# The delta rule's output projection in three fp32r products of split weights and split rows

## The reference, cut to what matters

```python
g = (hs @ Wg + bg).reshape(Bn, Ln, H, DV)
o = o * jax.lax.rsqrt(jnp.mean(o * o, axis=-1, keepdims=True) + EPS)
o = o * onorm_w * _silu(g)
o = o.reshape(Bn, Ln, H * DV) @ Wo + bo
...
x = x + _L0_attn_ref(_layernorm(x, axis=-1), ...)
```

## Time and profile before

| | us |
|---|---|
| median of 3 runs | 2178.61 |
| lowest and highest of them | 2173.72, 2178.92 |
| time of the profiled execution | 2174.62 |
| its span, from first to last instruction | 2172.6 |

### The profile page before, as it was taken

The page is one execution under the profiler, slowest core; times in us unless marked ns, Lnnn a source line. Parts: engine busy times, 40 slices in busy tenths (PEclk is TensorE's granted clock), DMA queues, the critical chain, the costliest instruction groups (busy, mean ns, idle before and its releaser), DMA issues. The chain is left out here.

```text
span 2172.6 us, 22255 instructions
## 1 busy us (share of the span) xinstructions
PE 1700.4 (78%) x7383; PEld 1173.6 (54%) x7383; DVE 1178.3 (54%) x2499; ACT 689.4 (32%) x1388; POOL 90.6 (4%) x262
## 2 busy tenths in 40 slices
PE   5999999999987999930940005971999999999993
PEld 2577777777765777720310004551666666666662
DVE  2233344333432258899999993332655555555553
ACT  1222222222212454430000003111555555555551
POOL 0000000000000000000211110002000000000003
PEclk9999999999987999975975556985999999999997
DMA  2100000000003234552200005205551554054104
GB/s 89 30 23 22 22 26 25 22 22 22 22 0 120 65 51 49 82 81 53 97 0 0 0 0 147 53 1 202 204 179 35 179 179 165 35 179 165 35 15 126
DMA packets 116295, 153.30 MB, mean 71 GB/s; under 512 B 47025, under 2 KB 67889, under 8 KB 116209
## 3 DMA queue, kind: packets, MB, share of 16 engines
q1 hardware_dynamic: 110336, 137.81, 21.9%
q0 software_dynamic: 2560, 8.39, 1.2%
q10 hardware_dynamic: 3312, 6.03, 0.7%
HBM read 250.58 MB, written 31.39 MB: 130 GB/s over the span
## 5 line engine op out<-in xcount | busy, mean ns | idle before, releaser
L1399 DVE TENSOR_TENSOR gl<-w_gu,gh 128x2048 fp32r<-128x2048 f32 x138 | 290.7, 2107 | 34.5 <-ACT gh L1346 34.5
L1346 ACT CAST gh<-w_gu 128x2048 fp32r<-128x2048 f32 x138 | 242.2, 1755 | 64.6 <-DMA w_gu<-in_up_proj 54.6
L1311 PE MATMUL bank<-w_d,hT 128*128 128x512 f32 x506 | 242.1, 597 | 9.3 <-ACT hT L1370 9.3
L1288 PE MATMUL bank<-gh,xh 128*128 128x512 f32 (+1 forms) x552 | 219.5, 398 | 12.1 <-DVE xl L1390 11.9
L1290 PE MATMUL bank<-gh,xl 128*128 128x512 f32 (+1 forms) x552 | 207.3, 376 | 0.0
L1289 PE MATMUL bank<-gl,xh 128*128 128x512 f32 (+1 forms) x552 | 206.3, 374 | 0.0
L964 PE MATMUL bank<-o_v,o_outw 128*128 128x64 f32 x256 | 36.3, 311 | 215.4 <-DMA o_v<-scratch_v_rows 215.4
L1413 DVE TENSOR_TENSOR hid<-silu,bank 128x256 f32<-128x256 f32 x138 | 55.1, 399 | 263.0 <-ACT silu L1359 262.8
L309 PE MATMUL bank<-ctxT,xa_wkv 128*128 128x257 f32 x768 | 176.8, 386 | 5.2 <-DMA ctxT<-in_ctxT 4.3
L316 PE MATMUL bank<-xa_wkv,ctxT 128*128 128x512 f32 x384 | 170.0, 592 | 0.0
L417 DVE COPY probT<-bank 128x512 f32<-128x512 f32 x64 | 41.3, 686 | 224.3 <-PE bank L336 224.3
(11 more groups left out here) (237 smaller groups left out, 2626.2 us busy)
## 6 DMA issues: line engine op xcount, KB each, us to landing
w_gu<-in_gate_proj SPq DMA_DIRECT2D x46, 1024.0 KB
w_gu<-in_up_proj SPq DMA_DIRECT2D x46, 1024.0 KB
w_d<-in_down_proj SPq DMA_DIRECT2D x46, 1024.0 KB
w_gu<-in_gate_proj SPq DMA_DIRECT2D x23, 768.0 KB
w_gu<-in_up_proj SPq DMA_DIRECT2D x23, 768.0 KB
w_d<-in_down_proj SPq DMA_DIRECT2D x23, 768.0 KB
ctxT<-in_ctxT SPq DMA_DIRECT2D x32, 385.5 KB, 3.3
scratch_gram<-gram SPq DMA_DIRECT2D x8, 768.0 KB, 3.3
```

What stands on the lines that cost most here:

```text
L1288: pe.matmul(bank, xh[s % 2][:, k, :], hi, start=(k == 0), stop=False)
L1311: mm = pe.matmul(bank, hT[n % 2][:, c, :], w_d[:, b * (BLK // P) + c, :], start=(b == 0 and c == 0), stop=(b == NB - 1 and c == cs[-1]))
L1346: nc.scalar.copy(gh[n % RING][:, :, :, 0:bw].rearrange("p k a f -> p (k a) f"), w_gu[:, :, :, b * BLK:b * BLK + bw].rearrange("p k a f -> ...
L1399: nc.vector.tensor_tensor(gl[n % RING][:, :, :, 0:bw].rearrange("p k a f -> p (k a) f"), w_gu[:, :, :, b * BLK:b * BLK + bw].rearrange("p ...
```

## The change

`oT` and `wo` are each split in two fp32r tensors, a high one (the value rounded by a cast) and a low one (the rest), and each float32 product is replaced by three fp32r products: high by high, high by low, low by high. Four things go with it.

1. At the start ScalarE waits for `w_in` and casts the whole of `wo` (128 x 4096) to `wo_hi`; VectorE waits for that and writes `wo_lo`, ahead of its eight bias adds.
2. ScalarE's copy of a turned bank now writes fp32r (`oT_hi`). VectorE has a new pair of instructions per tile, `split_turned(t-1)`, with 512 elements per partition each, which read the same bank and `oT_hi` and write `oT_lo`. They stand in its program behind the sum of squares of tile t and ahead of the add of tile t-1.
3. TensorE's products of a tile wait for `oT_low`, which VectorE counts, where they waited for `oT_done`, which ScalarE counts.
4. `o_sq`, both `o_g` and `wo` move into the space of `G`. The order of the transfers stays.

```diff
-def outputs(nc, d, ps, ident, x_nat, gate):
+def outputs(nc, d, ps, ident, x_nat, gate, spare):
...
-        o_sq = sb("o_sq", [P, H, DK])
-        o_g = [sb(f"o_g{s}", [P, H, DK]) for s in range(2)]
-        oT = [sb(f"o_gT{s}", [P, HC, P]) for s in range(2)]
+        o_sq = spare[:, 0:H * DK].rearrange("p (h k) -> p h k", h=H)
+        o_g = [spare[:, (s + 1) * H * DK:(s + 2) * H * DK].rearrange("p (h k) -> p h k", h=H) for s in range(2)]
+        sbr = lambda name, shape: ctx.enter_context(nc.sbuf_tensor(name, shape, F32R))
+        wo_hi, wo_lo = sbr("wo_hi", [P, HC, C]), sbr("wo_lo", [P, HC, C])
+        wo = spare[:, 3 * H * DK:3 * H * DK + HC * C].rearrange("p (c n) -> p c n", c=HC)
+        oT_hi, oT_lo = ([sbr(f"o_gT_{n}{s}", [P, HC, P]) for s in range(2)] for n in ("hi", "lo"))
...
                     if t:
-                        pe.wait_ge(oT_done, 2 * t)
+                        pe.wait_ge(oT_low, 2 * t)
...
                     if t == 0:
-                        pe.wait_ge(w_in, W_IN)
+                        pe.wait_ge(wo_split, 2)
...
                         if c % 4 == 0:
-                            pe.wait_ge(oT_done, 2 * t + c // 4 + 1)
-                        mm = pe.matmul(ps[Y_BANK + s], oT[s][:, c, :], wo[:, c, :], start=(c == 0), stop=(c == HC - 1))
+                            pe.wait_ge(oT_low, 2 * t + c // 4 + 1)
+                        pe.matmul(ps[Y_BANK + s], oT_hi[s][:, c, :], wo_hi[:, c, :], start=(c == 0), stop=False)
+                        pe.matmul(ps[Y_BANK + s], oT_hi[s][:, c, :], wo_lo[:, c, :], start=False, stop=False)
+                        mm = pe.matmul(ps[Y_BANK + s], oT_lo[s][:, c, :], wo_hi[:, c, :], start=False, stop=(c == HC - 1))
...
                 act.wait_ge(consts, 1)
+                act.wait_ge(w_in, W_IN)
+                nc.scalar.copy(wo_hi[:, :, :], wo[:, :, :]).then_inc(wo_split, 1)
+
                 def take_turned(t):
-                    if t == 0:
-                        act.wait_ge(w_in, W_IN)
...
-                        nc.scalar.activation(oT[t % 2]...
+                        nc.scalar.activation(oT_hi[t % 2]...
...
-                dve.wait_ge(w_in, W_IN)
+                dve.wait_ge(wo_split, 1)
+                nc.vector.tensor_tensor(wo_lo[:, :, :], wo[:, :, :], wo_hi[:, :, :].bitcast(F32), ALU.subtract).then_inc(wo_split, 1)
                 for t in range(NT):
                     nc.vector.tensor_tensor(x_nat[:, t, :], x_nat[:, t, :], bo[:, :], ALU.add).then_inc(x_bias, 1)
+
+                def split_turned(t):
+                    if t >= 2:
+                        dve.wait_ge(y_done, t - 1)
+                    for x in range(2):
+                        dve.wait_ge(oT_done, 2 * t + x + 1)
+                        nc.vector.scalar_tensor_tensor(oT_lo[t % 2][:, 4 * x:4 * x + 4, :].rearrange("p c n -> p (c n)"), ps[T_BANK + x],
+                                                       w_norm[:, 0:1], oT_hi[t % 2][:, 4 * x:4 * x + 4, :].rearrange("p c n -> p (c n)").bitcast(F32),
+                                                       ALU.mult, ALU.subtract).then_inc(oT_low, 1)
...
                     nc.vector.tensor_reduce(ss[:, :], o_sq[:, :, :], AX.X, ALU.add).then_inc(ss_done, 1)
                     if t:
+                        split_turned(t - 1)
                         add(t - 1)
...
+                split_turned(NT - 1)
                 add(NT - 1)
```

More of the change, by code:

```diff
@@ L916, in outputs @@
         sem = lambda name: ctx.enter_context(nc.semaphore(name))
-        wo, w_norm, bo, eps = sb("wo", [P, HC, C]), sb("w_norm", [P, 1]), sb("bo", [P, C]), sb("o_eps", [P, 1])
+        w_norm, bo, eps = sb("w_norm", [P, 1]), sb("bo", [P, C]), sb("o_eps", [P, 1])
         outw, v_row = [sb(f"o_outw{s}", [P, H, P]) for s in range(2)], [sb(f"o_v{s}", [P, H, DK]) for s in range(2)]
-        o_sq = sb("o_sq", [P, H, DK])
-        o_g = [sb(f"o_g{s}", [P, H, DK]) for s in range(2)]
-        oT = [sb(f"o_gT{s}", [P, HC, P]) for s in range(2)]
+        o_sq = spare[:, 0:H * DK].rearrange("p (h k) -> p h k", h=H)
[4 more added lines that the diff above has]
+        oT_hi, oT_lo = ([sbr(f"o_gT_{n}{s}", [P, HC, P]) for s in range(2)] for n in ("hi", "lo"))
+        wo_split, oT_low = sem("wo_split"), sem("oT_low")
         ss, rms, inv = sb("o_ss", [P, H]), sb("o_rms", [P, H]), [sb(f"o_inv{s}", [P, H]) for s in range(2)]
@@ L1011, in take_turned @@
                         act.wait_ge(turned, 2 * t + x + 1)
-                        nc.scalar.activation(oT[t % 2][:, 4 * x:4 * x + 4, :].rearrange("p c n -> p (c n)"), ps[T_BANK + x], ACT.Copy,
+                        nc.scalar.activation(oT_hi[t % 2][:, 4 * x:4 * x + 4, :].rearrange("p c n -> p (c n)"), ps[T_BANK + x], ACT.Copy,
                                              scale=w_norm[:, 0:1]).then_inc(oT_done, 1)
@@ L1067, in delta_rule @@
             recurrence(nc, d, ps, xnT, G, gt, phi, wz, rf, gate)
-            outputs(nc, d, ps, ident, x_nat, gate)
+            outputs(nc, d, ps, ident, x_nat, gate, G[:, :, :, :, :].rearrange("p s i e n -> p (s i e n)"))
 SCRATCH = {"v_last": (B, C), "gram": (TOK, H * 3 * N), "gates": ((NG + 1) * H, TOK),
```

## The result

The changed kernel is slower: 2206.72 us median against 2176.16 for the kernel before in the same measurement, ratio 1.0136, 95% interval 1.0111 to 1.0162. One of the four executions of the changed kernel took 9877 us; nothing in the other three (2203.5 to 2207.5, median 2205.95) answers to it, and it is left out of the ratio, though not of the median of 2206.72. The forecast was 2202, range 2188 to 2208; the profiled execution has a span of 2204.2 us, 31.6 more than before.

The account below looks back on a forecast made before the run. TensorE was taken to bound the steady tiles. Terms +7.4, +4.2, -0.7 and +14 gave +24.9 us: 2199.5 on the profiled run's 2174.6, 2203.5 on the median; forecast 2202, range 2188 to 2208.

Parts of the forecast that it names:

- The products: Each tile's projection: three fp32r products take 0.69 us against 0.867 for a float32 one, saving 1.42 us a tile.
- The row split: Steady tiles: VectorE's split, queued behind the sum of squares, starts products 2.1 us later; tile 13.2 us at full clock.
- The weight split: Stage start: cast 3.6 us and subtraction 4.4 us in series ahead of the bias adds; first product 8.2 us later.
- the cast's lower end: Stage start: at 0.72 ns an element, from the gate activations, ScalarE's cast would take 3.1 us, not 3.6.
- mix(2): TensorE's mix of tile 2, behind the first tile's products: starts 7.4 us later, the sum's start term.
- The clock: TensorE's clock falls in the longer idle of most tiles: 2.0 us each for seven tiles, +14 us; chance 0.74.
- -0.7: Last tile: the split only follows ScalarE, +0.75 us, and the products save 1.42 us.
- The sum: Whole stage: +7.4 start, +4.2 tiles at full clock, -0.7 last tile, +14 clock, so +24.9 us; later stages unchanged in length.
- The rival on the other side: Steady tiles: split directly behind ScalarE's copy, tile 0.8 us shorter, no clock fall, -6.3 us; split or weights hidden: 0.08.

Follow-up runs that it names:

- no_row_split: Changed kernel without VectorE's split of the rows; the third product takes oT_hi in place of oT_lo: 2176.52 us, ratio 1.0002 to the kernel before.
- turn_first: Changed kernel with all engines reordered: TensorE does transposes of t, mix of t+2, products of t; bias adds one a tile: 2161.4 us, ratio 0.9935.
- split_ahead: Changed kernel with VectorE's row split moved ahead of the sum of squares: 2191.53 us, ratio 1.0069 to the kernel before.
- filled: Changed kernel with three unneeded float32 products (one in the last tile) in TensorE's idle, none in the first tile: 2185.78 us, ratio 1.0045.
- row_split_only: Kernel before plus only VectorE's row split and TensorE's wait for it; products stay float32, weights unsplit: 2198.97 us, ratio 1.0103.
- pool_low: Changed kernel with wo_lo computed by GpSimd instead of VectorE; bias adds wait for the landing alone: 2201.9 us, ratio 1.0114.
- turn_first_f32: Same order of engines as turn_first, with float32 products and no cast or splits: 2168.24 us, ratio 0.9959 to the kernel before.

## Why the prediction was right

*The products.* 24 starts of 0.23 us at the full clock, one record each; -1.4 us a tile, confirmed by no_row_split (11.08) and by the two turn_first kernels (1.39).

*The row split.* The forecast was a first product 2.1 us later behind VectorE's sum, with one half's split at 0.69. The trace has an idle of 3.10, 2.14 more, and 1.40 us for the pair. split_ahead shows that the queue decides, filled that the tile without the clock's part is 13.15 (13.2 forecast).

*The weight split.* Cast 3.6 and subtraction 4.4, measured 3.60 and 4.43. No row given shows the 0.72 ns an element of the cast's lower end; the cast took 0.88. The first product was forecast 8.2 later in the stage, measured 8.7; the difference is the landing, which came 6.98 us behind the first mix, where it had been 6.41. mix(2) +7.4 forecast, +8.0 measured.

*The clock.* Falls in seven of seven tiles, 2.0 us each forecast, 2.1 in each of six by filled; in the last tile, where the sum has -0.7 and one fall, +0.8 was measured. Until those runs this term, the largest, rested on one idle in the trace, and the same trace has a longer one that the prediction doesn't name. Behind the stage, with wide products ahead of it, TensorE is idle for 4.00 us at the full clock, and the clock falls only in the stretch after:

```profile
1436.40:1440.40 4.00, 0.00 (x0) 0.00 (x0) 3.66 (x6) 0.00 (x0) 0.00 (x0) 1.00 0.00 0
1440.40:1444.20 3.80, 0.00 (x0) 0.00 (x0) 3.42 (x16) 0.21 (x1) 0.00 (x0) 0.54 0.00 0
```

So the length of an idle doesn't decide by itself. The forecast also counted what stood ahead of the idle, mix and transposes; these rows fit that, but no run changed it alone. That the falls need no fp32r is shown by row_split_only. Why the same idle costs a fall in each tile of the changed kernel and not in two of those with float32 isn't settled. The count of seven was thus in part luck.

*The sum.* +24.9 forecast for the stage, +25.6 measured. The span grew by 31.6, though, and the medians by 30.6: about 6 us lie outside the stage, where the prediction has nothing, since later stages were not to change. This is why 2206.72 lies 4.7 us above the forecast and near the upper end of its range, with the stage forecast to 0.7 us. In the profiled executions the time outside the stage is 2059.3 before and 2065.3 after; in the eight experiments, whose code outside the stage is the same, it runs from 2059.4 (filled) to 2066.1 (pool_low), with 2065.1 for turn_first. Of the 6 us, 1.5 lie ahead of the stage and 4.5 behind it. Two parts of the latter can be seen. TensorE's wait for the router's transfer grew from 2.79 to 4.11 us, and the router's products behind it ran wholly at the half clock after and partly at the full one before.

```profile
1453.45 0.72 PE L1133 MATMUL bank<-router,xnT 128*128 128x8 f32 x5 [2.79 <-DMA router<-in_router_w]
...
1453.45:1466.50 13.05, 13.05 (x64) 12.95 (x64) 0.00 (x0) 0.00 (x0) 0.34 (x11) 0.53 0.00 1
```

```profile
1482.25 1.02 PE L1152 MATMUL bank<-router,xnT 128*128 128x8 f32 x4 [4.11 <-DMA router<-in_router_w]
...
1482.25:1496.07 13.82, 13.82 (x64) 13.73 (x64) 0.00 (x0) 0.00 (x0) 0.00 (x0) 0.50 0.00 0
```

The kernel before by itself scatters as widely (2172.3 to 2179.5 over 13 executions), so most of this can be scatter between executions. But the traces lean one way: behind the stage the three kernels with float32 products (before, row_split_only, turn_first_f32) take 735.5, 736.8 and 737.0 us, the seven with fp32r products 737.0 to 740.8; and no_row_split, with a stage 3.4 us shorter, has in ten executions the time of the kernel before. So some 3 us may belong to the change. With one trace of each kernel that isn't shown, and its cause is open.

The rival on the other side, the split inside VectorE's idle, named the right place: it took another order of TensorE, not only of VectorE, to get there.

## What to carry to other kernels

A cheaper product is worth its saving only where the operands' preparation is off the path: here 1.4 us a tile were paid for with 2.1 us of waiting for a place late in another engine's queue, and with 2.1 more for the clock. Count an idle of TensorE twice, once as time and once as what the clock costs behind it; if the idle can't be removed, filling it with work that nobody needs is better than leaving it. Best is to put another tile's matmuls, already in the program, between producer and consumer.

## What the runs showed of the hardware

- An idle of TensorE of 0.96 us between narrow matmuls (mix and transposes) and a stream of wide ones kept the clock at 1.00 in the six tiles of the kernel before and of no_row_split; one of 1.89 to 1.98 us lost it in the same six tiles of split_ahead. Its price was 1.7 us a tile, almost that of 3.10 us of idle (2.1).
- The fall can come when TensorE is busy again: in split_ahead about 1 us into the wide products.
- The length of an idle isn't all: 4.00 us of idle behind wide products are at 1.00 in the kernel before. In its last tile, which has no mix, an idle of 2.20 us ahead of the transposes and 0.49 behind them kept the clock; 2.20 and 1.35 us lost it in the last tile of the changed kernel, of split_ahead and of row_split_only. In the last two tiles of turn_first 1.35 us behind transposes alone kept it.
- One GpSimd tensor_tensor of 4096 elements (9.87 us, where VectorE takes 4.43) stopped a VectorE tensor_tensor with two inputs in SBUF for 5.6 us, and neither those that read a bank nor a reduction.
- scalar_tensor_tensor from a bank with an fp32r result took 0.70 us for 512 elements, as tensor_tensor does (0.69).
